# Opening of a twelve-stage decoder kernel: order of the first loads, their waits, and the input's norms in two halves

## What is computed

```
x_in    = concatenate([mem, layernorm(x)], axis=1)      # 64 + 256 tokens for each of 8 items
out_swa = _swa(x_in, wq, wk, wv, wo)                    # 4 heads of 64, window of 128 tokens
grads   = grad(0.5 * sum((mlp(params, x_in) - out_swa) ** 2))   # params = w1, b1, w2, b2; HID = 1024
upd     = (1 - alpha) * params - theta * grads
out_mem = mlp(upd, x_in)
g1, g2  = sigmoid(out_swa @ lin1.T), sigmoid(out_mem @ lin2.T)
return (g1 * out_swa + g2 * out_mem)[:, 64:, :]
```

## Time and profile before

| | us |
|---|---|
| median of 3 timed executions | 3306.61 |
| lowest and highest | 3302.45, 3312.01 |
| profiled execution | 3305.28 |
| its span, first to last instruction | 3303.5 |
| PE busy | 2986.0 (90%) |
| DVE busy | 1881.9 (57%) |
| ACT busy | 1236.1 (37%) |
| mean granted clock of PE | 0.949 of full speed |

### The profile page before, as it was taken

The page is one execution under the profiler, slowest core; times in us unless marked ns, Lnnn a source line. Parts: engine busy times, 40 slices in busy tenths (PEclk is TensorE's granted clock), DMA queues, the critical chain, the costliest instruction groups (busy, mean ns, idle before and its releaser), DMA issues.

```text
span 3303.5 us, 52207 instructions
## 1 busy us (share of the span) xinstructions
PE 2986.0 (90%) x20631; PEld 1986.9 (60%) x20671; DVE 1881.9 (57%) x6433; ACT 1236.1 (37%) x1935; POOL 452.5 (14%) x470
## 2 busy tenths in 40 slices
PE   5999999989898978888888899997999999998988
PEld 3666766865555546555555556565666677765653
DVE  4434443699999356674677768674244443334455
ACT  1222212336564523223333457743333333223443
POOL 0010010124342300000010236510000000000000
PEclk9999999989998999989999769998999999998999
DMA  3000000010000000000000011010000000000000
GB/s 123 1 1 0 1 1 1 1 51 1 1 1 1 32 31 1 1 5 1 1 1 1 18 34 25 12 39 26 1 1 0 1 0 1 1 1 1 9 1 26
DMA packets 21725, 37.76 MB, mean 11 GB/s; under 512 B 2084, under 2 KB 19685, under 8 KB 20456
## 3 DMA queue, kind: packets, MB, share of 16 engines
q1 hardware_dynamic: 20664, 34.02, 3.0%
q10 hardware_dynamic: 816, 0.39, 0.0%
HBM read 26.81 MB, written 2.10 MB: 9 GB/s over the span
## 4 chain that ended last, share of the span: by engine, by line
PE 73%; DVE 19%; ACT 5%; issue 3%; SPq 1%; DMA 0%; DVEq 0%; POOL 0%; ACTq 0%; POOLq 0%
PE ps L386 42%; DVE arena L539 4%; PE ps L585 3%; ACT arena L620 2%; PE ps L2968 2%; PE ps L2276 2%; PE ps L2987 2%; PE ps L2230 2%; PE ps L487 2%; PE ps L1506 2%; PE ps L632 2%; PE ps L673 2%; DVE arena L1844 1%; PE ps L524 1%; PE ps L2841 1%
## 5 line engine op out<-in xcount | busy, mean ns | idle before, releaser
L386 PE MATMUL ps<-weights,arena 128*128 128x256 f32 (+4 forms) x2480 | 700.0, 431 | 24.0 <-ACT arena L1653 5.6
L386 PE MATMUL ps<-arena,weights 128*128 128x256 f32 (+4 forms) x1726 | 562.6, 474 | 35.9 <-DMA fp_bias<-in_fp_bias 27.2
L386 PEld LDWEIGHTS ps<-weights,arena 128*128 128x128 f32 (+1 forms) x2480 | 465.3, 198 | 191.3 <-issue 93.1
L386 PEld LDWEIGHTS ps<-arena,weights 128*128 128x128 f32 (+1 forms) x1726 | 319.3, 193 | 241.4 <-issue 155.3
L386 PE MATMUL ps<-arena 128*128 128x256 f32 (+4 forms) x1618 | 428.0, 418 | 6.0 <-ACT arena L4496 1.5
L386 PEld LDWEIGHTS ps<-arena 128*128 128x128 f32 (+2 forms) x1618 | 298.8, 188 | 116.5 <-issue 76.0
L620 ACT ACTIVATE arena<-ps 77x2048 f32<-77x2048 f32 (+1 forms) x112 | 210.0, 1875 | 170.4 <-PE ps L585 157.1
L539 DVE TENSOR_REDUCE arena<-ps 128x16 f32<-128x1232 f32 (+2 forms) x96 | 179.1, 1866 | 153.7 <-PE ps L524 50.3
L1844 DVE MATCH_REPLACE8 arena<-arena 128x77 f32<-128x77 f32 x1024 | 214.4, 225 | 0.0
L801 POOL TENSOR_TENSOR x<-x,weights 128x512 f32<-128x512 f32 x32 | 43.7, 1367 | 1243.9 <-DVE arena L767 1196.4
L2243 ACT ACTIVATE arena<-ps 128x1536 f32<-128x1536 f32 x128 | 185.7, 1452 | 72.8 <-PE ps L2232 66.4
(11 more groups left out here) (410 smaller groups left out, 4508.7 us busy)
## 6 DMA issues: line engine op xcount, KB each, us to landing
arena<-arena SPq DMA_DIRECT2D x156, 32.0 KB
weights<-in_w_L_attn SPq DMA_DIRECT2D x1, 4608.0 KB, 19.2
weights<-in_w_L_ffn SPq DMA_DIRECT2D x1, 3848.0 KB, 11.6
weights<-in_w_L_xattn SPq DMA_DIRECT2D x3, 1024.0 KB, 6.3
weights<-in_w_L_ffn SPq DMA_DIRECT2D x1, 3072.0 KB, 10.0
x<-in_x SPq DMA_DIRECT2D x1, 2048.0 KB, 8.5
weights<-in_w_L_xattn SPq DMA_DIRECT2D x1, 2048.0 KB, 7.4
out<-x SPq DMA_DIRECT2D x8, 256.0 KB, 2.2
```

Of the source, the lines that this page charges most:

```text
L386: ins = k.nc.tensor.matmul(out, lhsT, rhs, start=start and i == 0, stop=i == n - 1)
```

## The change

The semaphores x_loaded and mem_loaded are gone; qkv_loaded (memT and the first 1536 columns of the weights, which are wq, wk, wv) and early_loaded (tiles 0 to 7 of the input, ident, identb, the masks from swa0 on, and b12) take their place, and the other loads of the opening count on const_loaded. PE waits for qkv_loaded ahead of the memory projections, for early_loaded ahead of the memory scores, for the rest of the weights ahead of the output product, and for const_loaded ahead of the loop. ACT waits for const_loaded ahead of the loop, DVE ahead of alpha and theta; POOL waits as before. The memory scores stand ahead of item 0's transposes on PE. On DVE the norms are split: statistics, aggregates and Newton steps of tiles 0 to 7 in the opening, with the memory unit's copies between statistics and aggregates; the statistics of tiles 8 to 15 in round 0 and their aggregates and Newton steps in round 1, both ahead of the dw2 updates. The bias rows follow the memory unit's window_o_vector. Nothing else in the twelve stages is changed.

```diff
--- before.py
+++ after.py
@@ -333,6 +334,33 @@
+def first_norms_plan(k):
+    steps = 3 + RSQRT_STEPS
+    return Bag(sig=Signals(k.signals, "L0_attn", 1, 1, dve_step=steps, n_step=steps), parts=[None, None])
+
+
+def first_stats_vector(k, dve, s, part):
+
+    s.parts[part] = Chain(dve, s.sig, 0, 0, ("dve_step", "n_step")[part])
+    hold(k, dve, "vector")
+    for t in range(part * TILES // 2, (part + 1) * TILES // 2):
+        ins = k.nc.vector.bn_stats(k.stats[:, 6 * (SPARE + t):6 * (SPARE + t + 1)], k.xs[:, SPARE + t, :])
+    s.parts[part].link(ins)
+
+
+def first_norms_vector(k, dve, s, part):
+
+    v, ch, first, last = k.nc.vector, s.parts[part], part * TILES // 2, (part + 1) * TILES // 2
+    hold(k, dve, "vector")
+    for t in range(first, last):
+        ins = v.bn_aggr(k.norm[:, t, :], k.stats[:, 6 * (SPARE + t):6 * (SPARE + t + 1)])
+    ch.link(ins)
+    var = k.var[:, first:last]
+    ch.link(v.tensor_scalar(var, k.norm[:, first:last, 1:2].rearrange("p t o -> p (t o)"), LN_EPS, None, ALU.add))
+    rsqrt(k, ch.link, k.rstd[:, first:last], var, k.newton[:, first:last])
     ch.close()
 
 
@@ -3173,22 +3201,24 @@
     ins.then_inc(*s.memory.up("mT"))
 
 
-def L0_attn_tensor(k, pe, s):
-    pe.wait_ge(k.mem_loaded, 64)
-    enter(k, pe, s.wm)
+def L0_attn_tensor(k, pe, s, const_loaded, n_const):
+    pe.wait_ge(k.qkv_loaded, 32)
     m = s.mem
     window_qk_tensor(k, pe, s, m)
     window_v_tensor(k, pe, s, m)
     first = s.units[0]
+    pe.wait_ge(k.early_loaded, 80)
+    window_scores_tensor(k, pe, s, m, 0)
     window_zT_tensor(k, pe, s, first)
-    window_scores_tensor(k, pe, s, m, 0)
     pe.wait_ge(*s.setup.at("ready", 0, 0, 1))
     window_probs_tensor(k, pe, s, m, 0)
     window_outputs_tensor(k, pe, s, m, 0)
     window_qk_tensor(k, pe, s, first)
     window_oT_tensor(k, pe, s, m)
     window_v_tensor(k, pe, s, first)
+    pe.wait_ge(*k.loaded["L0_attn"])
     window_out_tensor(k, pe, s, m)
+    pe.wait_ge(const_loaded, n_const)
     for p in range(B + 1):
         g = [tile_of(s, None)] if p == 0 else [tile_of(s, 2 * p - 2), tile_of(s, 2 * p - 1)]
         pair = Bag(sig=s.pair if p else s.pm, n=max(p - 1, 0))
...
@@ -3402,19 +3433,19 @@
     for tile in (s.v, s.v_mem):
         v.memset(tile[:, :, :, SD_:SVW], 1.0)
     v.memset(s.keep, 0.0).then_inc(*s.setup.up("ready"))
-    dve.wait_ge(x_loaded, 16)
-    norms_vector(k, dve, s.norms)
+    dve.wait_ge(k.early_loaded, 80)
+    first_stats_vector(k, dve, s.norms, 0)
+    window_kv_vector(k, dve, s, m)
+    first_norms_vector(k, dve, s.norms, 0)
     window_z_vector(k, dve, s, first)
-    dve.wait_ge(const_loaded, n_const)
-    dve.wait_ge(k.mem_loaded, 64)
-    bias_rows_vector(k, dve, s)
-    window_kv_vector(k, dve, s, m)
     window_top_vector(k, dve, s, m, 0)
     window_o_vector(k, dve, s, m, 0)
+    bias_rows_vector(k, dve, s)
     window_kv_vector(k, dve, s, first)
     weights = ((flat(s.w1), w_of(k, "L0_attn", "w1T")), (flat(s.w2), w_of(k, "L0_attn", "w2T")))
     dve.wait_ge(*s.setup.at("ready", 0, 0, 1))
     dve.wait_ge(*k.loaded["L0_attn"])
+    dve.wait_ge(const_loaded, n_const)
     v.tensor_scalar(s.minus, scalar_of(k, "theta"), -1.0, None, ALU.mult)
     v.tensor_scalar(s.keep, scalar_of(k, "alpha"), -1.0, 1.0, ALU.mult, ALU.add).then_inc(*s.setup.up("kept"))
     dve.wait_ge(*s.setup.at("kept", 0, 0, 1))
@@ -3444,6 +3475,10 @@
             window_o_vector(k, dve, s, u, 1)
         if p:
             grad_g_vector(k, dve, s, g[1])
+        if p == 0:
+            first_stats_vector(k, dve, s.norms, 1)
+        if p == 1:
+            first_norms_vector(k, dve, s.norms, 1)
         for j in range(4):
             grad_dw2_vector(k, dve, s, pair, j)
         for j in range(4):
...
-        constants = [(k.ctxT, "ctxT"), (k.ident, "ident"), (k.identb, "identb"), (k.pick, "pick"), (k.masks, "masks"), (k.cols, "cols"),
-                     (k.ones, "ones"), (k.fp8_kernel_t, "fp8_kernel")]
-        n_const = 16 * (len(constants) + 2)
+        constants = [(k.ctxT, "ctxT"), (k.pick, "pick"), (k.cols, "cols"), (k.ones, "ones"),
+                     (k.fp8_kernel_t, "fp8_kernel")]
+        n_const = 16 * (len(constants) + 6)
...
                 n, m, _ = sizes[st]
-                    sp.dma_start(k.slot[st][:, AT.get(st, 0):AT.get(st, 0) + n], a["w_" + st][:, :]).then_inc(sem, 16)
+                    skip = QKV if st == "L0_attn" else 0
+                    sp.dma_start(k.slot[st][:, AT.get(st, 0) + skip:AT.get(st, 0) + n], a["w_" + st][:, skip:n])\
+                        .then_inc(sem, 16)
                 if m:
                     sp.dma_start(k.rowslot[st][0:1, row_start[st]:row_start[st] + m], a["r_" + st][:, :])\
                         .then_inc(sem, 16)
@@ -4757,14 +4794,23 @@
                     sp.dma_start(spread_of(k, st, name), a[st + "_" + name].unsqueeze(0).broadcast_to([P, D]))\
                         .then_inc(sem, 16)
 
-            sp.dma_start(k.xs[:, SPARE:SPARE + TILES, :], a["x"].rearrange("t p d -> p t d")).then_inc(x_loaded, 16)
+            half, window = TILES // 2, k.maskpos["swa0"][0]
+            sp.dma_start(first.zT_all[:, :, B * SEQ:B * SEQ + MEM], a["memT"].rearrange("(c p) t -> p c t", p=P))\
+                .then_inc(k.qkv_loaded, 16)
+            sp.dma_start(k.slot["L0_attn"][:, 0:QKV], a["w_L0_attn"][:, 0:QKV]).then_inc(k.qkv_loaded, 16)
+            sp.dma_start(k.xs[:, SPARE:SPARE + half, :], a["x"][0:half, :, :].rearrange("t p d -> p t d"))\
+                .then_inc(k.early_loaded, 16)
+            sp.dma_start(k.ident[:, :], a["ident"][:, :]).then_inc(k.early_loaded, 16)
+            sp.dma_start(k.identb[:, :], a["identb"][:, :]).then_inc(k.early_loaded, 16)
+            sp.dma_start(k.masks[:, window:], a["masks"][:, window:]).then_inc(k.early_loaded, 16)
+            sp.dma_start(first.b12[0:3, :], a["b12"].unsqueeze(0).broadcast_to([3, HID + D])).then_inc(k.early_loaded, 16)
             load("L0_attn")
-            sp.dma_start(first.zT_all[:, :, B * SEQ:B * SEQ + MEM], a["memT"].rearrange("(c p) t -> p c t", p=P))\
-                .then_inc(k.mem_loaded, 16)
-            sp.dma_start(first.z_mem[0:MEM, :], a["mem"][:, :]).then_inc(k.mem_loaded, 16)
-            sp.dma_start(first.b12[0:3, :], a["b12"].unsqueeze(0).broadcast_to([3, HID + D])).then_inc(k.mem_loaded, 16)
+            sp.dma_start(first.z_mem[0:MEM, :], a["mem"][:, :]).then_inc(const_loaded, 16)
+            sp.dma_start(k.xs[:, SPARE + half:SPARE + TILES, :], a["x"][half:TILES, :, :].rearrange("t p d -> p t d"))\
+                .then_inc(const_loaded, 16)
+            sp.dma_start(k.masks[:, 0:window], a["masks"][:, 0:window]).then_inc(const_loaded, 16)
             sp.dma_start(first.b2_all, a["b12"][HID:HID + D].unsqueeze(0).broadcast_to([P, D]))\
-                .then_inc(k.mem_loaded, 16)
+                .then_inc(const_loaded, 16)
```

19 lines of the change are left out of this document (10 added, 9 removed).

## The result

The changed kernel ran in 3286.99 us, the median of eight executions (3282.54 to 3295.30), beside 3305.01 us for the kernel before (eight executions, 3302.45 to 3312.01): a ratio of 0.9949, with a 95% interval of 0.9939 to 0.9959. That is 18.0 us less, by the interval 14 to 20; forecast were 3288.3 us and a gain of 18.3. The profiled execution took 3287.19 us.

The account below looks back on a forecast made before the run. The opening's latency, 0 to 49.09 us, was taken as the bound. Loop start -18.3, second-half norms 0, clock 0: 3305.28 becomes 3287.0, plus 1.3 to the median, 3288.3 us; range 3281 to 3298.

Parts of the forecast that it names:

- What bounds the kernel: Opening, 0 to 49.09 us: latency with hardly any work, so time taken out comes off the span one for one.
- Landing: Opening loads: 2223 KB in seven early requests land by 10.0 us, range 9 to 11.5, when DVE's first operation comes.
- DVE's chain and the first item: Opening, from landing: DVE's half of the norms gives z at 17.2, first item's q and k product at 21.6 us.
- The two paths: Into the loop: PE's products ready at 30.75 us, DVE's bias rows at 30.55, as good as equal.
- The shift: Loop start over the batch items: 30.75 instead of 49.09 us, 18.3 us less.
- The slower rival: Before the loop: the wait for all constants ends after 30.75 us and delays it, up to 3321 us; chance 0.02.
- The memory round: Loop's first round: second-half statistics, 2.66 us on DVE, cost 0 with 0.8 us of cover left, 2.3 without cover.
- the prediction's own test: Memory round: fourth dw2 update again 35.6 us behind the loop's start; if later, the cost of the second-half norms is wrong.
- step 4: Memory and next rounds: the second half of the norms costs 0; uncovered, 2.3 + 2.5 us.
- The next round: Round after the memory round: second-half aggregates and chain, 3.0 us on DVE, cost 0, at most 2.5.
- Clock: PE, opening and first round: clock unchanged; up to 4 us lost before the loop; afterwards 3.6 gained or some 3 lost.
- The sum: Whole kernel: -18.3 + 0 + 0 us against 3305.28 gives 3287.0, so the median is forecast at 3288.3 us.

Follow-up runs that it names:

- experiment 1: Two edits of the changed kernel: PE, ACT and DVE wait for all constants at start, 3307.24 us (1.0015); other weights issued before the early requests, 3300.41 us (0.9979).
- experiment 6: Three edits of the changed kernel: 1280 KB of weights ahead of the constants, 3291.25 us; 19 unread PE products, 3296.68; three bias-row operations moved earlier, 3295.13.
- Experiment 5: Changed kernel with ACT's wait for the constants one call earlier, ahead of the copy of the memory output; one execution, 3296.56 us.
- experiment 4: Two edits of the changed kernel: second-half aggregates and Newton chain moved to the memory round, 3297.45 us; or, in the next round, ahead of the first gradient product, 3299.29.
- order back: Changed kernel with the seven early requests issued behind the 3840 KB of other weights again; 3300.41 us, ratio 0.9979.
- norms earlier: Changed kernel with the second half's aggregates and Newton chain in round 1 moved ahead of the first gradient product; one timing, 3299.29 us.
- spare products: Changed kernel with 19 PE products of 128x256, results unread, in PE's idle spells of the opening; one timing, 3296.68 us.
- the last experiment: Changed kernel with ACT's wait earlier, bias rows split, first item's v product behind the loop's first products, 12 plus 3 unread PE products; 3288.08 us, ratio 0.9944.

## Why the prediction was right, point by point

- *What bounds the kernel:* right. The opening was latency, and 17.7 us out of it made 18.0 in the median. Neither of the two runs of experiment 1 keeps more than half of the gain.
- *Landing:* 10.70, expected 10.0 with 9 to 11.5. The bytes by the input's row were right to 0.7 us. The Trainium skill (DMA: Bandwidth & Descriptors, "Anatomy of one DMA — SWDGE (gpsimd) path") has a fit for transfers issued by GpSimd, by which it would have been 8.0; this queue doesn't follow it. PE's first matrix came at 6.02, as said.
- *DVE's chain and the first item:* 22.05 for the q and k product, expected 21.6. From the landing it took 11.35 us, the sum had 11.6.
- *The two paths:* PE 31.36 (30.75), bias rows 30.89 (30.55), nearly equal as said, and experiment 6 shows the one as the bound in after and the other in a kernel with PE held up. From landing to loop it took 20.66 us, the sum had 20.75. The shift was 17.7 instead of 18.3; the 0.6 is about what the landing came late.
- *The slower rival:* the constants land at 27.0 in the one kernel where they are the bound at their old place in the order, as at 27.16 before, and in after by estimate between 26.3 and 28.7, though SP was now held 10.38 us at one request instead of 7.35. The hold cost the loop nothing, as argued.
- *The memory round:* the cover of the statistics was as said (1.2 us of slack left, expected 0.8), but the fourth update came 36.8 us behind the loop's start, not 35.6, and by the prediction's own test something in step 4 was wrong. It was not the norms. The missed term is ACT's added wait, 1.3 us, which the prediction didn't price at all: it looked at what is queued behind the new waits of DVE and PE, and not at ACT's table load, which had run for free in the wait for PE. Experiment 5 shows it twice, in the sigmoid's 1.3 us and in two rounds of the same clock that differ by 1.34.
- *The next round:* cost 0, as said, but with the step at 4.7 us instead of 3.0, since POOL held DVE's two tensor_scalars (experiment 4). It stayed covered: both rounds are 57.80 us.
- *Clock:* taken as unchanged. The memory round has 0.92 now and had 0.91. That this held is partly luck: in three kernels whose code in this round is after's (order back, norms earlier, spare products) it was 0.84 in the trace kept and the round 43.9 to 44.0 us, 3 longer, which lies inside the bounds given.
- The sum thus had three misses, +0.6 at the loop's start, +1.2 in the memory round, and -1.5 us between 130 us and the end, where the code is the same (16.6 ahead, then 18.1): a low spell at 350.8 us that before's trace has and after's has not. They cancel, and that is luck. So is it that the forecast lies within 1.3 us of the median, where the gain is known to 14 to 20 us.

## What to carry to other kernels

A new order of loads was worth nothing with all engines waiting for the last of them at their start (1.0015), and waits by first use, with the work moved to suit them, were worth less than half without the order (0.9979); the gain came from both together. What is moved out of an opening has to go where its engine waits anyway, and the way to see it is a later operation in the same round that still waits for another engine. When a wait is added to an engine, look at the instructions right behind it, a table load among them: one that used to run for free may inherit the next wait.

## What the runs showed of the hardware

- *GpSimd holds a VectorE tensor_scalar for whole instructions, several in a row.* 128x8 took 1.57 instead of 0.17 us, and a 128x512 one 6.56 or 10.01 us while one tensor_tensor and two or three MEMSETs ran on POOL; a like one right behind it (L976) takes 0.43 us. The lock that the Trainium skill describes (SBUF — State Buffer, "SBUF: two separate sides"; see under 4) fits; that back-to-back GpSimd instructions can shut DVE out for 10 us is what these traces add. Not every operation is held: eight-tile statistics beside POOL's two took 2.70 us (62.12 to 64.82 in after), as without it (2.71).
- *The pace of PE in the opening.* The first item's 16 q and k products took 5.25 to 6.56 us where PE had stood before, and 3.72 us in the three kernels where it had been kept busy. In the kernel before, the windows around them give a clock of 0.59 and 0.70; in all the others they give 1.00, at 3.72 and at 6.56 us alike. So in the opening the duration tells the pace, and the clock column doesn't.
- *A low spell follows idle time.* In after PE is busy for 0.53 us of the 4 from 36.0, and from 40.0 on the window has half the clock, 1.2 GHz:

```profile
36.00:40.00 4.00, 0.53 (x5) 0.53 (x6) 1.76 (x2) 2.16 (x2) 0.00 (x0) 0.94 0.00 0
40.00:46.00 6.00, 6.00 (x31) 3.86 (x30) 3.80 (x4) 2.51 (x3) 0.00 (x0) 0.50 0.01 3
```

With spare products in that round (the last experiment) there was none, and the round took 3.0 us less than in after. All of that lies in PE's products of this stretch:

```profile
33.91 0.69 DVE L2946 COPY arena<-ps 128x512 f32<-128x512 f32 x1 [3.85 <-PE ps L414]
34.52 1.21 DVE L3087 TENSOR_TENSOR arena<-ps,arena 64x1024 f32<-64x1024 f32 x1
...
37.95 3.67 PE L3018 MATMUL ps<-weights,arena 128*64 128x256 f32 x16
```

The sigmoid's product (L3087) is 7.0 us behind the loop's start (27.53), no sooner than after's 6.8: what the earlier table load gained is lost to the copy of v, which was moved in front of it. From PE's next products to the end of the 16 (L3018 here, L3015 in after) it takes 5.84 us, in after 8.97, and those 16 alone 3.67 instead of 5.18.
